# Rotary attention with 16 heads: the order of the last two projections in a pair's second sequence

## The reference

```python
qkv = jnp.einsum('bse,ef->bsf', x, W_qkv)
q, k, v = (qkv[:, :, 0], qkv[:, :, 1], qkv[:, :, 2])   # after a reshape to (.., 3, 16, 64)
q = rotary_embedding(q, seq_len, HEAD_DIM)
k = rotary_embedding(k, seq_len, HEAD_DIM)
scores = jnp.einsum('bqhd,bkhd->bhqk', q, k) * scale
scores = jnp.where(mask, scores, NEG_INF)
weights = jax.nn.softmax(scores, axis=-1)
out = jnp.einsum('bhqk,bkhd->bqhd', weights, v)
return jnp.einsum('bsf,fe->bse', out, W_out)
...
x = _layernorm(x + _L3_attn_ref(x, L3_attn_W_qkv, L3_attn_W_out), axis=-1)
```

## Time and profile before

| | before |
|---|---|
| median of 3 runs | 3455.29 us (3452.86 to 3456.1) |
| the profiled execution | 3453.05 us |
| its span | 3451.3 us |
| PE busy over the span | 2777.9 us (80%) |
| DVE busy | 1960.1 us (57%) |
| ACT busy | 1387.4 us (40%) |
| POOL busy | 1272.5 us (37%) |

### The profile page before, as it was taken

One profiled execution on the slowest core, in us unless ns is written; L12 is line 12 of the kernel. 1 busy time (PEld: TensorE's weight loads), 2 busy tenths in 40 slices (PEclk: granted clock), 3 DMA queues, 4 the chain that ended last, 5 costly groups with the idle time before them and its releaser, 6 DMA issues. The chain is left out here.

```text
span 3451.3 us, 78570 instructions
## 1 busy us (share of the span) xinstructions
PE 2777.9 (80%) x31785; PEld 1976.5 (57%) x31785; DVE 1960.1 (57%) x5133; ACT 1387.4 (40%) x3112; POOL 1272.5 (37%) x1365
## 2 busy tenths in 40 slices
PE   6980466577667699799899996798979999988986
PEld 3550233265443477556699985566456666665665
DVE  5987988406456344366554444464755555544665
ACT  3540455416334455344422222454133434334554
POOL 3440243317221111345323333453743333324555
PEclk9995677659678899899899998898999999998998
DMA  3000000030000000000000000001000000000000
GB/s 99 3 2 2 1 1 1 1 107 1 1 6 1 32 2 2 39 3 3 8 1 1 1 1 1 17 2 42 0 5 2 2 2 2 2 2 8 2 2 25
DMA packets 24454, 37.29 MB, mean 11 GB/s; under 512 B 569, under 2 KB 21185, under 8 KB 23233
## 3 DMA queue, kind: packets, MB, share of 16 engines
q1 hardware_dynamic: 24096, 32.30, 2.9%
HBM read 30.07 MB, written 2.23 MB: 9 GB/s over the span
## 5 line engine op out<-in xcount | busy, mean ns | idle before, releaser
L1193 POOL TENSOR_TENSOR L_attn__qk<-L_attn__turned 128x512 f32<-128x512 f32 x128 | 161.5, 1273 | 352.7 <-DVE L_attn__turned L1302 352.7
L4218 PE MATMUL psum<-L_ffn__e_hT,weights 128*128 128x256 f32 x1024 | 244.4, 382 | 0.0
L777 DVE TENSOR_REDUCE L_xattn__nm<-psum 128x8 bf16<-128x1024 f32 x128 | 156.4, 1224 | 149.4 <-PE psum L970 143.0
L1302 DVE TENSOR_TENSOR L_attn__turned<-psum,weights 128x1024 f32<-128x1024 f32 x128 | 153.4, 1219 | 144.7 <-PE psum L1409 141.7
L4218 PEld LDWEIGHTS psum<-L_ffn__e_hT,weights 128*128 128x128 f32 x1024 | 186.5, 192 | 20.5
L4072 DVE TENSOR_TENSOR L_ffn__e_a<-L_ffn__e_sg,psum 128x512 f32<-128x512 f32 x128 | 87.9, 687 | 176.2 <-ACT L_ffn__e_sg L4064 176.2
L4064 ACT ACTIVATE L_ffn__e_sg<-psum 128x512 f32<-128x512 f32 x128 | 76.5, 598 | 258.4 <-PE psum L4218 258.4
L717 ACT ACTIVATE L_xattn__pT<-psum 128x1024 f32<-128x1024 f32 x128 | 124.0, 1021 | 59.0 <-PE psum L998 59.0
L4231 PEld LDWEIGHTS psum<-weights,L_ffn__e_a 128*128 128x128 f32 x1024 | 134.4, 191 | 7.2 <-DVE L_ffn__e_a L4072 0.7
L1409 PE MATMUL psum<-L_attn__xT,weights 128*128 128x256 f32 x512 | 136.2, 399 | 1.9 <-DVE L_attn__turned L1302 1.2
L4231 PE MATMUL psum<-weights,L_ffn__e_a 128*128 128x128 f32 x1024 | 135.0, 275 | 0.5 <-DVE L_ffn__e_a L4072 0.5
(11 more groups left out here) (677 smaller groups left out, 7613.3 us busy)
## 6 DMA issues: line engine op xcount, KB each, us to landing
L_xattn__toeplitz<-s4d_kernel SPq DMA_DIRECT2D x8, 1024.0 KB, 5.7
weights<-pack SPq DMA_DIRECT2D x1, 3328.0 KB, 10.5
weights<-pack SPq DMA_DIRECT2D x1, 3140.0 KB, 10.5
weights<-pack SPq DMA_DIRECT2D x1, 2370.0 KB, 9.2
out_dram<-X SPq DMA_DIRECT2D x1, 2048.0 KB, 8.7
weights<-pack SPq DMA_DIRECT2D x1, 1732.5 KB, 10.3
ctxT<-ctxT_in SPq DMA_DIRECT2D x1, 1536.0 KB, 22.0
weights<-pack SPq DMA_DIRECT2D x1, 1376.0 KB, 5.5
```

What stands on the lines that cost most here:

```text
L777: nc.vector.tensor_reduce(nm[:, n % 2, :].rearrange("p (g c) -> p g c", g=4)[:, 2 * u:2 * u + 2, 0:4], scores[u].rearrange("p g (i q) -> p ...
L1193: nc.gpsimd.tensor_tensor(qk[:, p % 2, u], turned[:, g % 2, :, 0:2 * P], turned[:, g % 2, :, 2 * P:4 * P], ALU.add).then_inc(qk_sb, 1)
L1302: nc.vector.tensor_tensor(turned[:, g % 2], proj[u % 2].unsqueeze(1).to_broadcast([P, 2, 4 * P]), k.w(name + "rope").rearrange("p (t q) -> ...
L4218: last = nc.tensor.matmul(bank[g % 2][:, 256 * c:256 * c + 256], k.w(name + w)[:, o:o + P], hT, start=True, stop=True)
```

## The change

The last projection of queries and keys (unit 7) moves on TensorE from behind the weighing to ahead of it, in odd sequences. Its rotation on VectorE moves from behind the reciprocal to ahead of it. On ScalarE the 16-bit copies of units 6 and 7 move from behind the eviction of the spread to ahead of it. GpSimd's order is as before. Even sequences, and the last pair, are as before. No instruction is added or removed and no wait is changed.

```diff
                     first = 4 * (n % 2)
-                    for u in range(first, first + 2 if p < LAST else 0):
+                    early = 2 if n % 2 == 0 else 4
+                    for u in range(first, first + early if p < LAST else 0):
                         cast(p + 1, u)
                     evict_over(n)
-                    for u in range(first + 2, first + 4 if p < LAST else 0):
+                    for u in range(first + early, first + 4 if p < LAST else 0):
                         cast(p + 1, u)
...
                         if more:
                             turn(p + 1, 6)
+                            turn(p + 1, 7)
                         inverted(n)
-                        if more:
-                            turn(p + 1, 7)
                         weighted(n)
...
                         if more:
                             project(p + 1, 6)
+                            project(p + 1, 7)
                         weigh(n)
-                        if more:
-                            project(p + 1, 7)
                         spread(n)
```

## The result

The changed kernel takes 3465.15 us (median of 9 runs, against 3455.10 for 9 runs of the kernel before beside it), a ratio of 1.0030 with a 95% interval of 1.0021 to 1.0039: 0.3% slower, where 3464.6 us was forecast. The profiled execution took 3465.52 us.

What follows compares the result with a forecast made beforehand. TensorE's in-order stream was taken as the bound; 0.67 us lost less 0.05 gained, 0.62 in each of 15 odd sequences, adds 9.3 us, giving 3464.6 us (0.27% slower), range 3456 to 3472.

Steps and rivals of the forecast that it cites:

- TensorE's stream is the path: In the changed stage TensorE's in-order stream bounds: busy 475.16 of 521 us, VectorE next with 292.83.
- the copies' idle time isn't to be had: Before the rough scores: moving the copies gains only 0.05 us per odd sequence, not the 1.17 us idle.
- The second projection ahead of the weighing costs 0.67 us: L1470 to L1484, odd sequences: one projection is free, the second lengthens the way from 1.59 to 2.26 us.
- Nothing is given back behind the weighing: L1484 to L1499: 4.06 us with or without a projection, since the reciprocal sets the spread's start.
- Rotation, sums and copies are hidden: VectorE, GpSimd, ScalarE: moved work costs nothing, with 1.2 us left before the reciprocal and 1.5 before the spread's eviction.
- The delay passes undiminished: From rough scores to the next sequence's scores: everything slides equally, no slack, 0.74 us idle time included.
- The second rival: Idle 0.74 us before the next scores takes up the delay: no change, 3454.5 to 3457 us; chance 0.08.
- The sum: Weighing 0.67 later less 0.05 gained: 0.62 us in each of 15 odd sequences, 9.3 us in all.
- The clock rival: A second hole of some 1.1 us per odd sequence lowers TensorE's clock: 18 us, 3483 us; chance 0.07.

Runs made afterwards that it cites:

- casts_only: Kernel before with only ScalarE's part of the change: copies of units 6 and 7 ahead of the spread's eviction; 3500.09 us, ratio 1.0130.
- both_behind: Kernel before, odd sequences: units 6 and 7 both projected behind the weighing and rotated behind the reciprocal; 3469.45 us, ratio 1.0053.
- even_late: Kernel before, even sequences: unit 1 projected behind the weighing, unit 2 behind the spread, with later rotations and copies; 3463.10 us, ratio 1.0023.
- after_v0: Changed kernel, odd sequences: first value piece projected ahead of the spread instead of behind it; 3486.88 us, ratio 1.0099.
- casts_v1: casts_only with the second value piece ahead of the next rough scores in odd sequences; 3480.59 us against the kernel before, ratio 1.0083.

## Why the prediction was right

- *TensorE's stream is the path, and the copies' idle time isn't to be had.* Right. Predicted 0.05 us, measured 0.04 (19.23 against 19.19). The rule of the Trainium skill (Perfetto Trace Analysis, section Optimization Strategy) that a dependency which ends a gap should be made to start sooner would have given 17.4 us, if the whole gap is put down to the releaser; here the releaser's name changed and the gap stayed, 1.17 us before and 1.13 after. The 15 waits behind these 17.4 us are not the 15 odd sequences, as the prediction has it, but 14 of them and the first even one; nothing in the sum hangs on it. casts_only, which moves that same releaser forward without its own producer, lost 45.7 us.
- *The second projection ahead of the weighing costs 0.67 us.* Right: a went from 1.59 to 2.27. both_behind shows from the other side that one projection is free there, and even_late takes the same 0.67 us back out of the even sequences' way to the weighing.
- *Nothing is given back behind the weighing.* Right: b is 4.05 with 1.08 us idle.
- *Rotation, sums and copies are hidden.* Right, with 1.53 us left before the eviction (1.5 predicted), and 2895.10 - 2893.66 = 1.44 us before the reciprocal (1.2 predicted). This holds only since the projection moves along: casts_only is the same copy order with the cover gone, and costs 1.88 us. No run moves the rotation alone, so that it is free is read from these rows.
- *The delay passes undiminished.* Right: 6.61 us from the rough scores to L1454 in both, the 0.74 us of idle time included. The second rival falls with it.
- *The sum.* 0.62 predicted, 0.63 measured for each sequence; 9.3 against 9.5 in the traces and 10.05 between the medians.
- *The clock rival.* Rightly discounted for this change: 1.00 throughout the stage. But its mechanism is real in this very stage. The Trainium skill (TensorE: Matmul & The Clock Gate, section A second HAM failure mode: psum-queue depth-cycling) describes a clock that swings with short and frequent pauses; the changed kernel's pauses of 1.1 us don't do it, those of 2.2 us in after_v0 did in 13 of 15 sequences. The last pair, from which the prediction took this rival, has a hole of 2.18 us beside the one of 1.08, so it is the like of after_v0 and not of the change. My price of 2.4 us for a fall was mostly too high: one fall cost 2.9, the other 31 of the three kernels 1.3 to 1.7.

Three expectations failed. In casts_only (29 us for 45.7) and after_v0 (no loss for 21 us more) I counted a longer idle time at its own length and left the clock out. In even_late the sign was wrong (3 to 9 us faster expected, 8.7 slower measured), because projection 5 waits 0.82 us for the bank that VectorE rotates late. For casts_v1 the result lies between the two forecasts.

## What to carry to other kernels

TensorE waits twice in an odd sequence here, and each wait hides one projection; a second one in the same place cost 0.67 and 0.78 us of its 0.86. So before moving work, read how long each wait is without it and with it, from rows where both orders exist. A releaser's name tells who came last, not how much could be won: look for the next wait behind it, here 0.13 us away. Independent work of the following stage belongs into a wait that another chain sets: such moves gave 1.2% here. Look at the granted clock after each move: filling one wait and so lengthening another lost 21 us (after_v0).

## What the runs showed of the hardware

The granted clock depends on how the idle time is laid out, not only on its sum. Two holes of 1.08 and 1.13 us with the spread and a piece of values between them left the clock at 1.00 in all 15 odd sequences of the changed kernel. One hole of 2.18 us (after_v0) was followed by a fall to the lower level in 13 of 15, a hole of 3.05 us (casts_only) in 11 of 15, and one of 2.2 us with two pieces of values ahead of it (casts_v1) in 8 of 15, each counted in one execution. In the last pair, the same in all 14 kernels, a hole of 2.1 to 2.2 us was followed by a fall in 24 of 28 cases, so a fall is likely there and not certain.

In the odd sequences of these three kernels each fall but one cost 1.3 to 1.7 us, because the output projection that comes next ran in part at 1.2 GHz, and in casts_only the pieces of values behind it too (granted clock 0.50 at 2922 to 2923 us). An edit that only shifted 1.1 us of idle time from one place to another so became 21 us.
